# Attention stage: turn and mix moved one block behind the scores, one softmax per block, PSUM banks shared out anew

## The chip, the cores and the metric

The kernel runs on one core of one Trainium2 chip. The metric is the device time of one execution in microseconds (us), lower is better; three runs of the kernel before were timed. TensorE (PE) has two clock levels here, 2.4 GHz (granted clock 1.00 in the views) and 1.2 GHz (0.50).

## What is computed

Two encoders feed an attention over N = 4 states for each of 1024 tokens; an interference stage and three dense layers follow. The attention stage is what the change touches:

```python
# TOK = 1024 tokens, N = 4 states, D = 512, H = 8 heads of HD = 64
qr = heads(sr @ Wq_r.T + bq_r); qi = heads(si @ Wq_i.T + bq_i)
kr = heads(sr @ Wk_r.T + bk_r); ki = heads(si @ Wk_i.T + bk_i)
vr = heads(sr @ Wv_r.T + bv_r); vi = heads(si @ Wv_i.T + bv_i)
ar = einsum('bhnd,bhmd->bhnm', qr, kr) + einsum('bhnd,bhmd->bhnm', qi, ki)
ai = einsum('bhnd,bhmd->bhnm', qi, kr) - einsum('bhnd,bhmd->bhnm', qr, ki)
mag = sqrt(ar ** 2 + ai ** 2 + 1e-08) * HD ** (-0.5)
w = softmax(mag, axis=-1)                       # over the 4 states of one token
out_r = einsum('bhnm,bhmd->bhnd', w, vr); out_i = einsum('bhnm,bhmd->bhnd', w, vi)
attn_r = out_r @ Wo_r.T + bo_r; attn_i = out_i @ Wo_i.T + bo_i
```

## The kernel before

The program is six stages one after the other (constants, first layers, second layers, attention, interference, top), each with its own five instruction streams (TensorE = PE, VectorE = DVE, ScalarE = ACT, GpSimd = POOL, SyncE = SP) written out by hand and tied together by counting semaphores. There is no scheduler: each engine works its stream in the order in which it is written, so an instruction that waits holds up all that stands behind it on its engine.

**The attention stage** (`phase_attention`, L491) works on 16 blocks `b` of 64 tokens (256 columns: 64 tokens times 4 states). Inside a block, `m` = 0..3 stands for a pair of heads. Every dense product is made of three fp32r matmuls (`split3`, L50 to L52: high by high, low by high, high by low), and so every result that feeds another product is split into a high and a low half, by ACT and DVE. The pieces of a block are:

- `project(b, m)` on PE (lines L50 to L52 with `t_sx`): q and k for a pair of heads, 24 matmuls of 256 columns each. ACT reads q out of PSUM (`q_evac`, L618, 4 instructions), DVE reads k (`k_evac`, L708, 8 instructions).
- `values(b)`: v, four groups of 12 matmuls of 512 columns. ACT reads them out (L680).
- `score(b, m, h)` (L846): fp32 matmuls of q by k. ACT squares the result (L625).
- `softmax(b, m)` on DVE: add, mask, sum (L725, L729, L730); ACT root (L671); DVE maximum and difference (L735, L736); ACT exponent (L674); DVE sum, reciprocal (L739, L740), and the spread of the weights into `pd` (L744).
- `turn(b, m)` (L852) transposes `pd` on PE, ACT copies it out (`pt_evac`, L631), `mix(b, m)` (L865) multiplies it by v, ACT and DVE split the result (`o_high` L638, `o_low` L753).
- `project_out(b)`: the output projection (L50 to L52 with `t_ohi`), 96 matmuls, read out by `a_high` (L646, ACT) and `a_low` (L764, DVE), and stored by SP.

**Banks.** PSUM's eight banks are shared out in pairs: 0 and 1 for q, k, v and the output projection, 2 and 3 for the scores, 4 and 5 for `turn`, 6 and 7 for `mix`, so `turn` and `mix` each alternate between two banks.

**Order.** PE's body interleaves: `project(b, m+1)`, a score, `turn` of the pair before (`before(b, m)`), the second score, `mix` of the pair before; `values` and the output projection of block b-1 stand after m = 0. ACT and DVE follow in the same order. The 32 weight pieces are split into halves at the start of the stage and in block 0 (`pieces`). SP stores block b-1 before it loads block b+1 (`load_s`).

## Time and profile before

| | us |
|---|---|
| median of 3 runs | 3566.72 |
| lowest, highest | 3565.09, 3569.43 |
| span of the profiled execution | 3548.6 |
| median less that span | 18.1 |
| attention stage, first to last matmul | 1179.9 |
| one block of it | 71.6 |
| PE busy over the whole span | 3115.3 (88%) |
| DVE busy, ACT busy | 1652.0 (47%), 1168.9 (33%) |

The profiled execution's record gives its span alone and no device time of its own; the runs' median lies 18.1 us above it, for what is ahead of the first and behind the last instruction. A busy share is an average over six stages. What a change in the attention stage is worth is read from that stage, by what PE waits for in one block.

### The profile page before, as it was taken

How to read it: one execution, taken by the hardware profiler on the slowest of the kernel's cores; microseconds unless marked ns; L12 is line 12 of the kernel's file. 1: busy time of each engine (PE TensorE's matmuls, PEld its weight loads, DVE VectorE, ACT ScalarE, POOL GpSimd, SP SyncE). 2: the span in 40 equal slices, each digit the busy share in tenths (PEclk: the TensorE clock that was granted, in tenths of full speed). 3: DMA queues.
4: the chain of work that ended last, by engine and by line, in shares of the span. 5: the costliest groups of instructions: out<-in, count | busy, mean ns of one | idle time of the engine just before them, and what ended most of it. 6: DMA issues, size and time to landing. Idle time of an engine off the chain costs nothing. (4 is left out here: it accounts for less than half of the span.)

```text
span 3548.6 us, 45531 instructions
## 1 busy us (share of the span) xinstructions
PE 3115.3 (88%) x16160; PEld 2659.5 (75%) x16160; DVE 1652.0 (47%) x3027; ACT 1168.9 (33%) x1986; POOL 388.2 (11%) x345
## 2 busy tenths in 40 slices
PE   8999999996999899995889989898989598884586
PEld 6888888885888788874778878887878476763575
DVE  3222222226211341114665566556655579999322
ACT  3111111114211241114554555455555432332332
POOL 1000000001111110010000000000000244543100
PEclk9999999998999999997998989898989799997798
DMA  5222222214333333323212221122112553442210
GB/s 181 71 71 71 71 71 71 71 59 163 113 95 95 113 118 94 93 74 128 78 47 56 62 71 47 49 70 71 47 47 72 136 102 83 89 85 45 95 36 6
DMA packets 364201, 285.38 MB, mean 80 GB/s; under 512 B 280048, under 2 KB 280176, under 8 KB 364016
## 3 DMA queue, kind: packets, MB, share of 16 engines
q1 hardware_dynamic: 341488, 206.97, 21.6%
q0 software_dynamic: 22656, 77.67, 6.3%
q8 instruction: 33, 0.54, 0.1%
q14 instruction: 24, 0.20, 0.0%
HBM read 194.40 MB, written 90.18 MB: 80 GB/s over the span
## 5 line engine op out<-in xcount | busy, mean ns | idle before, releaser
L50 PE MATMUL banks<-a_whi,a_xhi 128*128 128x512 f32 x1152 | 449.9, 391 | 24.0 <-DVE a_wlo L175 17.6
L51 PE MATMUL banks<-a_wlo,a_xhi 128*128 128x512 f32 x1152 | 448.8, 390 | 0.0
L52 PE MATMUL banks<-a_whi,a_xlo 128*128 128x512 f32 x1152 | 448.8, 390 | 0.0
L50 PE MATMUL banks<-b_ghi,b_whi 128*128 128x512 f32 x1024 | 401.8, 392 | 9.9 <-DVE b_slo L383 8.6
L51 PE MATMUL banks<-b_glo,b_whi 128*128 128x512 f32 x1024 | 398.9, 390 | 0.0
L52 PE MATMUL banks<-b_ghi,b_wlo 128*128 128x512 f32 x1024 | 398.8, 389 | 0.0
L175 DVE TENSOR_TENSOR a_wlo<-a_wraw,a_whi 128x512 fp32r<-128x512 f32 x144 | 99.6, 692 | 577.2 <-ACT a_whi L161 577.2
L50 PE MATMUL banks<-t_sx,t_whi 128*128 128x256 f32 x1024 | 307.7, 300 | 36.8 <-DVE t_wlo L791 26.9
L161 ACT ACTIVATE a_whi<-a_wraw 128x512 fp32r<-128x512 f32 x144 | 90.9, 632 | 667.7 <-PE banks L52 628.9
L51 PE MATMUL banks<-t_sx,t_whi 128*128 128x256 f32 x1024 | 295.7, 289 | 0.0
L368 DVE TENSOR_TENSOR b_wlo<-b_wraw,b_whi 128x512 fp32r<-128x512 f32 x128 | 88.2, 690 | 444.8 <-ACT b_whi L320 444.6
L52 PE MATMUL banks<-t_sx,t_wlo 128*128 128x256 f32 x1024 | 294.5, 288 | 0.0
L708 DVE TENSOR_SCALAR t_ks<-banks,cols 64x256 f32<-64x256 f32 x512 | 247.4, 483 | 97.5 <-PE banks L52 86.4
L50 PEld LDWEIGHTS banks<-a_whi,a_xhi 128*128 128x128 f32 x1152 | 216.6, 188 | 72.0 <-issue 17.6
L52 PEld LDWEIGHTS banks<-a_whi,a_xlo 128*128 128x128 f32 x1152 | 216.6, 188 | 45.2
L51 PEld LDWEIGHTS banks<-a_wlo,a_xhi 128*128 128x128 f32 x1152 | 216.7, 188 | 44.8
L50 PEld LDWEIGHTS banks<-t_sx,t_whi 128*128 128x128 f32 x1024 | 203.5, 199 | 43.2 <-DVE t_wlo L791 27.5
L50 PEld LDWEIGHTS banks<-b_ghi,b_whi 128*128 128x128 f32 x1024 | 192.7, 188 | 54.9 <-DVE b_slo L383 13.1
L320 ACT ACTIVATE b_whi<-b_wraw 128x512 fp32r<-128x512 f32 x128 | 80.2, 628 | 458.2 <-PE banks L52 457.5
L50 PE MATMUL banks<-i_whi,i_ax 128*128 128x512 f32 x384 | 159.3, 415 | 72.6 <-ACT i_ng L1075 38.1
L52 PEld LDWEIGHTS banks<-b_ghi,b_wlo 128*128 128x128 f32 x1024 | 192.4, 188 | 40.1
L51 PEld LDWEIGHTS banks<-b_glo,b_whi 128*128 128x128 f32 x1024 | 192.7, 188 | 39.0
(192 smaller groups left out, 6208.8 us busy)
## 6 DMA issues: line engine op xcount, KB each, us to landing
a_wraw<-w_first SPq DMA_DIRECT2D x144, 256.0 KB, 2.6
b_wraw<-w_second SPq DMA_DIRECT2D x128, 256.0 KB, 2.7
t_sx<-s_scr SPq DMA_DIRECT2D x64, 512.0 KB, 5.5
a_scr<-t_at SPq DMA_DIRECT2D x256, 128.0 KB, 1.9
i_ax<-a_scr SPq DMA_DIRECT2D x64, 512.0 KB, 5.9
h_scr<-a_hst POOLq DMA_DIRECT2D x72, 256.0 KB, 2.7
b_hl<-h_scr POOLq DMA_DIRECT2D x16, 1024.0 KB, 6.0
s_scr<-b_shi POOLq DMA_DIRECT2D x32, 512.0 KB, 4.4
```

Of the source, the lines that this page charges most:

```text
L50: mm(out, ahi, bhi, start=first, stop=False)
L51: mm(out, ahi, blo, start=False, stop=False)
L52: return mm(out, alo, bhi, start=False, stop=last)
L161: act.activation(whi[:, k % SPL, :], wraw[:, k % RAW, :], ACT.Copy).then_inc(w_hi, 1)
L175: dve.tensor_tensor(wlo[:, k % SPL, :], wraw[:, k % RAW, :], whi[:, k % SPL, :].bitcast(F32), ALU.subtract).then_inc(w_split, 1)
L320: act.activation(whi[:, j % SPL, :, :].rearrange("p a n -> p (a n)"), wraw[:, j % RAW, :], ACT.Copy).then_inc(w_hi, 1)
L368: dve.tensor_tensor(wlo[:, j % SPL, :, :].rearrange("p a n -> p (a n)"), wraw[:, j % RAW, :], whi[:, j % SPL, :, :].bitcast(F32).rearrange ...
L708: ins = dve.tensor_scalar(ks[half(at_half), m % 2, h, part, :], b_qk[half(h), 1, e * C:(e + 1) * C], bcol(M_K + e, m, half(h)), float(sign ...
```

## The change

The reference is computed as before, with the same matmuls.

- **Banks.** Bank 0 alone for q, banks 1 and 2 for k, 3 and 4 for the scores, bank 5 alone for both `turn` and `mix` (`b_pm`), banks 6 and 7 for v and the output projection.
- **One block behind.** `turn` and `mix` of block b-1 run among the projections and scores of block b. In body b: projection of q, `turn(b-1, m-1)`, projection of k, `score(b, m-1)`, `mix(b-1, m-1)`, for m = 1..3; then `turn(b-1, 3)`, the first values, the last score, `mix(b-1, 3)`, the other values, and the output projection of b-1.
- **One softmax a block.** `softmax` falls apart: `pick` (add, mask, sum) for each pair of heads, then once a block `magnitude`, `shift`, `exponent` and `total` for all four pairs at once, and `spread` for each pair.
- **New waits.** `turn(b, m)` waits for `o_split` of the pair before it, since `mix` of that pair was read out of the same bank.
- **The end.** The last block's four turns and mixes run after the loop, one after the other.
- SP loads block b+1 ahead of the stores of block b-1, in two halves. GpSimd clears 11 old semaphores at the start of the second layers.

```diff
-        b_qk, b_sc, b_pt, b_mx = (g.ps[:, 2 * i:2 * i + 2, :] for i in range(4))
+        b_q = g.ps[:, 0, :]
+        b_k = g.ps[:, 1:3, :]
+        b_sc = g.ps[:, 3:5, :]
+        b_pm = g.ps[:, 5, :]
+        b_vo = g.ps[:, 6:8, :]
...
             def turn(b, m):
-                pe.wait_ge(step, b * 32 + (8 * m + 8))
+                pe.wait_ge(pd_made, b * 4 + (m + 1))
+                if not isinstance(b, int) or 4 * b + m >= 1:
+                    pe.wait_ge(o_split, b * 8 + 2 * m)
```

PE's body, which takes the place of the old one:

```diff
+            def body(b, first):
+                project(b, 0, 0)
+                project(b, 0, 1)
+                for m in range(1, KD):
+                    project(b, m, 0)
+                    if not first:
+                        turn(b - 1, m - 1)
+                    project(b, m, 1)
+                    score(b, m - 1)
+                    if not first:
+                        mix(b - 1, m - 1)
+                if not first:
+                    turn(b - 1, KD - 1)
+                values(b, 0)
+                score(b, KD - 1)
+                if not first:
+                    mix(b - 1, KD - 1)
+                for i in range(1, 4):
+                    values(b, i)
+                if not first:
+                    project_out(b - 1)
```

DVE's body:

```diff
+            def body(b, first):
+                k_evac(b, 0)
+                for m in range(1, KD):
+                    k_evac(b, m)
+                    pick(b, m - 1)
+                    if not first:
+                        spread(b - 1, m)
+                        o_low(b - 1, m - 1)
...
+                pick(b, KD - 1)
+                if not first:
+                    o_low(b - 1, KD - 1)
+                shift(b)
+                total(b)
+                spread(b, 0)
+                if not first:
+                    for m in range(KD):
+                        a_low(b - 1, m)
```

ACT's body up to the third pair, and PE's end of the stage:

```diff
+            def body(b, first):
+                q_evac(b, 0)
+                for m in range(1, KD):
+                    q_evac(b, m)
+                    if not first:
+                        pt_evac(b - 1, m - 1)
+                    square(b, m - 1)
+                    if not first:
+                        o_high(b - 1, m - 1)
+                    if first and m == 1:
+                        pieces(M_V * KD, M_O * KD)
+                    if first and m == 3:
+                        pieces(M_O * KD, NP)
...
             blocks(pe, body)
-            turn(NB - 1, KD - 1)
-            mix(NB - 1, KD - 1)
+            for m in range(KD):
+                turn(NB - 1, m)
+                mix(NB - 1, m)
             project_out(NB - 1, True)
```

DVE's stream before, in block 1 at the pair m = 1 (`t_olo` is the low half of the mixed result, `t_ks` the k read-out, `t_m` and `t_sc` the softmax's steps, `t_pd` the spread weights; x7 counts like instructions):

```order
313 L753 SCALAR_TENSOR_TENSOR t_olo<-banks,cols,t_ohi 64x256 [waits t_o_hi]
314 L753 SCALAR_TENSOR_TENSOR t_olo<-banks,cols,t_ohi 64x256 x3
315 L708 TENSOR_SCALAR t_ks<-banks,cols 64x256 [waits t_scored,t_projected]
316 L708 TENSOR_SCALAR t_ks<-banks,cols 64x256 x7
```

The low half of a pair stands right ahead of the next k read-out, and nothing that PE does on the way asks for it but a `mix` two pairs later.

DVE's stream after the change, in block 1 between one k read-out and the next:

```order
329 L749 TENSOR_SCALAR t_ks<-banks,cols 64x256 [waits t_projected,t_scored]
330 L749 TENSOR_SCALAR t_ks<-banks,cols 64x256 x7
331 L759 TENSOR_TENSOR t_m<-t_sq 128x512 [waits t_picked,t_squared]
332 L764 TENSOR_TENSOR t_m<-t_m,mask 128x512 [waits t_summed]
333 L768 TENSOR_REDUCE t_mg<-t_m 128x16 [waits t_mag_done,t_masked]
334 L798 SCALAR_TENSOR_TENSOR t_pd<-t_ex,t_inv,mask 128x128 [waits t_p_turned,t_inv_done]
335 L798 SCALAR_TENSOR_TENSOR t_pd<-t_ex,t_inv,mask 128x128 x3
336 L807 SCALAR_TENSOR_TENSOR t_olo<-banks,cols,t_ohi 64x256 [waits t_o_hi]
337 L807 SCALAR_TENSOR_TENSOR t_olo<-banks,cols,t_ohi 64x256 x3
```

The low half now stands last, behind the k read-out, the pick and the spread.

PE's stream before, in block 0 around the last two pairs of scores (`t_ks,t_qs` the scores, `ident,t_pd` the turn, `t_ptl,t_v` the mix):

```order
1912 L846 MATMUL banks<-t_ks,t_qs 128x2x128 [waits t_squared,t_k_read,t_q_read]
1913 L846 MATMUL banks<-t_ks,t_qs 128x2x128
1914 L852 MATMUL banks<-ident,t_pd 128x128 [waits t_step]
1915 L852 MATMUL banks<-ident,t_pd 128x128 x3
1916 L846 MATMUL banks<-t_ks,t_qs 128x2x128 [waits t_squared]
1917 L846 MATMUL banks<-t_ks,t_qs 128x2x128
1918 L865 MATMUL banks<-t_ptl,t_v 128x128 [waits t_v_read,t_pt_read]
1919 L865 MATMUL banks<-t_ptl,t_v 128x128 x3
```

The turn waits for its weights alone (`t_step`).

PE's stream after the change, in block 1 at the last turn:

```order
2126 L905 MATMUL banks<-t_ks,t_qs 128x2x128 [waits t_squared,t_k_read,t_q_read]
2127 L905 MATMUL banks<-t_ks,t_qs 128x2x128
2128 L905 MATMUL banks<-t_ks,t_qs 128x2x128 [waits t_squared]
2129 L905 MATMUL banks<-t_ks,t_qs 128x2x128
2130 L924 MATMUL banks<-t_ptl,t_v 128x128 [waits t_v_read,t_pt_read]
2131 L924 MATMUL banks<-t_ptl,t_v 128x128 x3
2132 L913 MATMUL banks<-ident,t_pd 128x128 [waits t_o_split,t_pd_made]
2133 L913 MATMUL banks<-ident,t_pd 128x128 x3
2134 L50 MATMUL banks<-t_whi,t_sx 128x512 [waits t_v_read,t_w_split]
```

Here the turn of the last pair follows at once on the mix of the pair before, and waits for `t_o_split` too; the 512-column values stand behind it.

## Rows read from the trace of the kernel before

**Rows 1.** Windows view: length, busy us of PE, PEld, DVE, ACT, POOL; PEclk; DMA.

```profile
1618.18:2798.04 1179.86, 1037.10 (x6656) 936.92 (x6656) 707.79 (x1748) 636.85 (x1174) 0.00 (x0) 0.90 0.21 59
1860.90:1932.54 71.64, 64.44 (x416) 58.32 (x416) 43.34 (x108) 38.97 (x72) 0.00 (x0) 0.90 0.22 59
```

**Rows 2.** Timeline of ACT: first values read-out of blocks 3 and 4.

```profile
1860.90 1.08 ACT L680 ACTIVATE t_v<-banks 128x512 f32<-128x512 f32 x2
...
1932.54 1.08 ACT L680 ACTIVATE t_v<-banks 128x512 f32<-128x512 f32 x2
```

**Rows 3.** Timeline of PE in one block: start, us, instruction, [idle before <-releaser].

```profile
1861.55 0.79 PE L50 MATMUL banks<-t_whi,t_sx 128*128 128x512 f32 x1 [3.14 <-ACT t_v L680]
...
1869.71 0.39 PE L52 MATMUL banks<-t_whi,t_sx 128*128 128x512 f32 x1
1869.94 0.28 PE L50 MATMUL banks<-t_ohi,t_whi 128*128 128x256 f32 x1
...
1881.25 0.28 PE L50 MATMUL banks<-t_sx,t_whi 128*128 128x256 f32 x1
...
1887.00 1.03 PE L846 MATMUL banks<-t_ks,t_qs 128*128 128x256 f32 x4
1887.87 0.60 PE L852 MATMUL banks<-ident,t_pd 128*128 128x128 f32 x4
1888.30 1.03 PE L846 MATMUL banks<-t_ks,t_qs 128*128 128x256 f32 x4
1889.23 1.16 PE L865 MATMUL banks<-t_ptl,t_v 128*128 128x128 f32 x8
1890.14 0.36 PE L50 MATMUL banks<-t_sx,t_whi 128*128 128x256 f32 x1
...
1903.28 3.78 PE L846 MATMUL banks<-t_ks,t_qs 128*128 128x256 f32 x8 [2.43 <-DVE t_ks L708]
```

**Rows 4.** Waits of PE from 1840 to 2760 us: total, times, longest.

```profile
PE banks L50 <- ACT t_v L680: 40.8, 13, 3.2
PE banks L846 <- DVE t_ks L708: 29.1, 12, 2.4
PE banks L865 <- ACT t_ptl L631: 15.6, 13, 1.2
```

**Rows 5.** Timeline of DVE in the same block.

```profile
1887.20 4.02 DVE L708 TENSOR_SCALAR t_ks<-banks,cols 64x256 f32<-64x256 f32 x8 [3.43 <-PE banks L52]
...
1895.78 1.14 DVE L744 SCALAR_TENSOR_TENSOR t_pd<-t_sc,mask 128x128 f32<-128x128 f32 x4
1897.11 2.00 DVE L753 SCALAR_TENSOR_TENSOR t_olo<-banks,cols,t_ohi 64x256 fp32r<-64x256 f32 x4 [0.18 <-ACT t_ohi L638]
1899.13 4.02 DVE L708 TENSOR_SCALAR t_ks<-banks,cols 64x256 f32<-64x256 f32 x8
1903.18 0.69 DVE L725 TENSOR_TENSOR t_m<-t_sq 128x512 f32<-128x512 f32 x1
...
1904.64 0.69 DVE L730 TENSOR_REDUCE t_sc<-t_m 128x16 f32<-128x512 f32 x1
```

**Rows 6.** Timeline of PE in the last stage: a gap, and the matmuls behind it.

```profile
3393.57 0.55 PE L50 MATMUL banks<-e_whi,e_rhi 128*128 128x256 f32 x1 [4.58 <-DVE e_rlo L1496]
...
3396.70 0.31 PE L52 MATMUL banks<-e_whi,e_rlo 128*128 128x256 f32 x1
```

**Rows 7.** Timeline of PE at the end of the attention stage.

```profile
2776.92 1.12 PE L852 MATMUL banks<-ident,t_pd 128*128 128x128 f32 x4 [4.00 <-DVE t_pd L744]
...
2784.89 0.55 PE L50 MATMUL banks<-t_ohi,t_whi 128*128 128x256 f32 x1 [4.09 <-issue]
```

**Rows 8.** Timeline of PE at the start of the stage, in block 0.

```profile
1625.79 0.58 PE L50 MATMUL banks<-t_sx,t_whi 128*128 128x256 f32 x1 [2.88 <-DVE t_wlo L791]
...
1647.08 0.79 PE L50 MATMUL banks<-t_whi,t_sx 128*128 128x512 f32 x1 [7.90 <-DVE t_wlo L791]
```

**Rows 9.** DMA issues: KB each, median us to landing.

```profile
t_sx<-s_scr SPq DMA_DIRECT2D x64, 512.0 KB, 5.5
```

More of the change, by code:

```diff
@@ L76, in phase_constants @@
         cols_in = s.sem("cols_in")
+        g.spent = [zeroed, made, cols_in]
         block = s.ctx.enter_context(nc.Block())
@@ L288, in load_h @@
                 pool.dma_start(hl[:, j % 2, :, :], src.rearrange("t p f -> p t f")).then_inc(h_loaded[j % 2], 16)
+            for old in g.spent:
+                pool.sem_clear(old)
             load_h(0, 0)
@@ L604, in _ @@
                 sp.dma_start(raw(i), g.w_pieces[PC_ATT + i]).then_inc(w_loaded[i % TR], 16)
-            blocks(sp, body)
+            reload(0)
+            reload(1)
+            store(0)
+            with sp.Fori(2, NB - 1) as b:
+                reload(b)
+                store(b - 1)
+            store(NB - 2)
             store(NB - 1)
@@ L709, in k_evac, with pick @@
                                                 bcol(M_K + e, m, half(h)), float(sign), ALU.add, ALU.mult)
                     ins.then_inc(k_read, 1)
-            def softmax(b, m, unit=None):
-                done = [0]
-                def link(ins):
-                    ins.then_inc(step, 1)
-                    done[0] += 1
-                    dve.wait_ge(step, b * 32 + (8 * m + done[0]))
+            def pick(b, m):
                 dve.wait_ge(squared, b * 8 + (2 * m + 2))
+                if not isinstance(b, int) or 4 * b + m >= 1:
+                    dve.wait_ge(picked, b * 4 + m)
@@ L768, in a_low @@
                     ins.then_inc(a_split, 1)
-            def before(b, m):
-                return (b, m - 1) if m else (b - 1, KD - 1)
-            def body(b, first, last):
-                for m in range(KD):
-                    if m < KD - 1:
-                        k_evac(b, m + 1)
-                    if first and m == 0:
-                        pieces(M_V * KD, M_O * KD)
-                    if first and m == 2:
-                        pieces(M_O * KD, NP)
-                    softmax(b, m, (b + 1, 0) if m == KD - 1 and not last else None)
-                    if not (first and m == 0):
-                        o_low(*before(b, m))
-                    if m == 0 and not first:
-                        for mm in range(KD):
-                            a_low(b - 1, mm)
             def pieces(i0, i1):
@@ L792, in pieces @@
                                       ALU.subtract).then_inc(w_split, 1)
+            def body(b, first):
[6 more added lines that the diff above has]
+                        o_low(b - 1, m - 1)
+                    if first and m == 1:
+                        pieces(M_V * KD, M_O * KD)
+                    if first and m == 3:
+                        pieces(M_O * KD, NP)
+                pick(b, KD - 1)
[5 more added lines that the diff above has]
+                if not first:
+                    for m in range(KD):
+                        a_low(b - 1, m)
             pieces(0, M_V * KD)
-            k_evac(0, 0)
             blocks(dve, body)
-            o_low(NB - 1, KD - 1)
+            for m in range(KD):
+                if m < KD - 1:
+                    spread(NB - 1, m + 1)
+                o_low(NB - 1, m)
             for m in range(KD):
@@ new lines, in values @@
+            def values(b, i):
+                pe.wait_ge(w_split, M_O * KD)
+                e, gr = i // 2, i % 2
+                if i >= 2:
+                    pe.wait_ge(v_read, b * 4 + (i - 1))
+                elif not isinstance(b, int) or b >= 2:
+                    pe.wait_ge(a_split, b * 8 - (10 - 2 * i))
+                elif b == 1:
+                    pe.wait_ge(v_read, 3 + i)
+                for k in range(KD):
+                    w = (M_V + e) * KD + k
+                    mm = split3(pe.matmul, b_vo[:, i % 2, :], sx[:, e, 0, gr, k, :], sx[:, e, 1, gr, k, :],
+                                whi[:, w, :], wlo[:, w, :], k == 0, k == KD - 1)
+                mm.then_inc(v_full, 1)
@@ new lines, in score @@
+            def score(b, m):
+                pe.wait_ge(q_read, b * 8 + (2 * m + 2))
+                pe.wait_ge(k_read, b * 16 + (4 * m + 4))
+                for h in range(2):
+                    if not isinstance(b, int) or 4 * b + m >= 1:
+                        pe.wait_ge(squared, b * 8 + (2 * m - 1 + h))
+                    for gr in range(NG):
+                        cols = slice(gr * P, (gr + 1) * P)
+                        out = b_sc[:, h, :].rearrange("p (a g c) -> p a g c", a=2, g=NG)[:, :, gr]
+                        mm = pe.matmul(out, qs[:, m % 2, h, cols], ks[:, m % 2, h, :, cols], start=True, stop=True)
+                    mm.then_inc(scored, 1)
```

307 lines of the change are left out of this document (144 added, 163 removed).

## The prediction, made before the changed kernel was run

> **What bounds the kernel now.** I read the page first, for the shares: PE is busy 88% of the span, DVE 47%, ACT 33%. That is a mean over six stages, so I went on to the windows view of the attention stage alone. It takes 1179.9 us from its first matmul to its last, with PE busy for 1037.1 and a granted clock of 0.90 [rows 1]. All sixteen blocks look alike: the first values read-out of one block stands 71.64 us behind that of the block before [rows 2]. So I cut out one such block. PE is busy 64.4 us of it and idle for 7.2, at a clock of 0.90 [rows 1].
>
> PE's timeline shows what a block holds at the upper clock level [rows 3]. Two projections and so 48 matmuls of 256 columns take 1881.25 to 1887.00, 5.75 us, or 2.88 for q and 2.88 for k alone. Half of a pair's scores is 0.87, a turn 0.43 (1887.87 to 1888.30), a mix 0.91 (1889.23 to 1890.14). The output projection is 1869.94 to 1881.25, 11.3. The 512-column matmuls of the values stand 0.23 apart (1869.71, 1869.94), so 48 of them are 10.9. The sum for a block is 8 x 2.88 + 8 x 0.87 + 4 x 0.43 + 4 x 0.91 + 10.9 + 11.3 = 57.5 us. The remaining 14.1 are 7.2 of idle time and 6.9 in which PE works at half clock.
>
> The view of the waits names the idle time [rows 4]: about 3.1 us a block for ACT's values read-out, 2.4 for the k read-out ahead of the last scores, 1.2 for ACT's copy of the turned weights. Behind the 3.14 us gap the 24 matmuls of the values take 1861.55 to 1869.94, 8.4 us in place of 5.45 [rows 3], which is PE at 1.2 GHz until shortly before their end; the rest of the 6.9 comes behind the other two waits, where eight score matmuls take 3.78 us. So the block is bound by PE, plus waits on DVE and ACT, plus the slow clock that follows each wait. This is what a change of order can win, or lose.
>
> **The change part by part.**
>
> *The three old waits* go. The values no longer share banks with q and k and stand behind a long run of PE work; the first two groups find free banks, and the v read-outs are no longer queued behind a softmax's two table loads. The copy of the turned weights has a whole k projection (2.88 us) to hide in, where 0.87 us of scores hid it. That would take 7.2 us of idle and 6.9 of slow clock off each block, if nothing took their place.
>
> *The new wait.* Turn and mix now share bank 5. `turn(b-1, m)` may write only when DVE has done `o_low` of the pair before. I walk DVE's queue from the moment T at which PE has issued its last matmul of a k projection. DVE starts its k read-out 0.20 later (1887.00 against 1887.20, [rows 3, 5]). The read-out's eight instructions take 4.05 (1899.13 to 1903.18), the pick 2.19 (three of 0.73), the spread 1.17 (1.14 and a step), `o_low` 2.02 (1897.11 to 1899.13) [rows 5], and I add 0.07 for the hand-over to PE. The turn can start at T + 9.7. In the same time PE has: two halves of scores 1.74, mix 0.91, the next q projection 2.88, so 5.53. It waits 9.7 - 5.5 = 4.2 us for the second turn and as much for the third. Ahead of the fourth turn there is no q projection, so PE has 2.65 of work and waits 7.05. What is queued behind it on PE is the k projection in the first two cases (and DVE's next k read-out waits for that, so the gap can't be made up), the values in the third. Sum: 4.2 + 4.2 + 7.0 = 15.4 us idle a block, for 7.2 before.
>
> *The clock.* Each of these gaps is longer than the 3.14 us one, behind which PE ran slow for most of 8.4 us and lost 2.9 [rows 3]. The other bound is the 4.58 us gap in the last stage: the matmuls behind it are slow from 3393.57 to 3396.70 [rows 6], 15 of them 0.21 apart in place of 0.12, so 1.4 lost. I take 2.3 a gap, between the two and nearer to the first, which lies in this stage. Three gaps: 6.9 us a block, with 4.2 and 8.4 as ends.
>
> *One softmax a block.* It takes six of eight table loads and most of the small steps off ACT and DVE. DVE is busy 43.3 us of a block and ACT 39.0 [rows 1], less than a block of 57.5. The load was not the bound, the order is. Worth nothing beside the above. The once-a-block steps wait for each other while PE has 8.2 us of values and 11.3 of output projection to do; they need four small DVE steps of under 0.3 each and two table loads on ACT, about 5 us together.
>
> *SP.* Block b+1's second half is loaded when the last values are done and lands in about 5.5 us [rows 9], under 11.3 us of output projection. If that cover were gone it would cost its excess, microsecond for microsecond, once a block. The stores queue behind four issues, and their first data comes later than that anyway.
>
> *Block 0.* It has no turns and mixes: 8 x 2.88 + 6.96 + 10.9 = 40.9 of work. Before, it had waits for weight pieces of 2.88 and 7.90 [rows 8], and others. Now the values come last, so the 7.90 goes; the first 2.9 stays; I expect about 4 where the q read-out stands behind eight pieces on ACT, and about 4 where the v read-outs stand behind the last eight. With 4 for the clock: 56.
>
> *The end.* The four turns and mixes of block 15 have nothing beside them. The chain turn, copy, mix, `o_high`, `o_low` is in the trace once: from the turn at 2776.92 to the first matmul of the output projection at 2784.89, 7.97 us at the lower clock [rows 7]. Four of them are 32, and the output projection 13.2 with a slow start (it took 2784.89 to 2798.04). So 45.
>
> *The 11 cleared semaphores* stand ahead of the second layers' first load. No row shows such an instruction on GpSimd; between 0 and 1 us, I take 0.5.
>
> **The sum.** A block: 57.5 + 15.4 + 6.9 = 79.8 us, for 71.6. The stage: 56 + 15 x 79.8 + 45 = 1298, for 1179.9. With the 0.5: 119 us more. The trace's span of 3548.6 becomes 3667, and with the 18.1 us by which the median lies above the span, 3686 us.
>
> **The rivals.**
>
> *The bank wait is hidden (faster).* The mechanism would be that `o_low` is done before PE comes to the turn. It decides at 5.5 us for two of the turns and 2.65 for the third. Then all waits are gone, a block is 57.5, and the stage 56 + 863 + 45 = 964: 216 less, 3351 us. For it: DVE has only some 40 us of work in a block. Against it: the walk gives 9.7, the k read-out alone takes 4.05 of it, and DVE works in order. The Trainium skill (TensorE: Matmul & The Clock Gate, HAM oscillation) reports of one kernel that double-buffering PSUM brought no further gain once its loop kept PE fed; by that, one bank in place of two and two would cost nothing, and this rival's time would come out. No row of this trace shows two engines sharing a single bank in turns. 4 in 100.
>
> *The clock stays up (no change).* If gaps of 4 and 7 us did not lower the clock, the 15 x 6.9 us and some 12 at the ends fall away: 3571 us, 0.1% from now. The new idle time alone would then be what the old idle time and slow clock were together. For it: nothing but that the pattern of work differs. Against: the gap of 3.14 us was followed by slow matmuls, 13 times in the stretch of [rows 4] at the same place. 5 in 100.
>
> *The load comes late.* If the second half of the next block's data took 13 us in place of 5.5, the first projections would wait 2 us in 15 blocks: 3716 us. 4 in 100.
>
> *The slow clock lasts.* With the gaps about every 13 us, PE may stay at half clock through the first values too, another 2 to 3 us a block: 3725 us. 4 in 100.
>
> **How the numbers follow.** My forecast has 83 in 100. Its own bounds: the clock from 4.2 to 8.4 a block is -40 and +22 us; the walk's durations, by 0.3 in each of three gaps, 14; block 0 and the end 8. That makes 3635 to 3722. The range 3620 to 3725 takes in the late load and leaves out the rivals at 3351 and 3571. Faster by over 0.2% has 4 in 100 (the first rival); within 0.2%, which is about what a measurement of this kernel can tell from no change, 5 (the second); slower by over 0.2% has 91.
>
> **What would show it right or wrong.** The profile after should show PE idle before the turn (L913), with `o_low` (L807) as releaser, three times a block from block 1 on, at some 4.2, 4.2 and 7.0 us; values read-outs 80 us apart; no wait of the values for L677 over 1 us; DVE going from k read-out to `o_low` without a gap; and four waits of some 4 us each for `o_low` at the end of the stage. The clock in one block should be near 0.8. I would be wrong if DVE's chain has gaps in it (then slower still), if the third wait is not the longest, or if the matmuls behind the waits run at 0.12 us apart.

## The result: slower by 3%, at the place that the walk named

| | before | after |
|---|---|---|
| median of 4 runs, us | 3566.01 | 3673.91 |
| lowest, highest | 3565.09, 3569.43 | 3672.49, 3677.1 |
| ratio after / before | | 1.0331, 95% interval 1.0273 to 1.039 |
| span of the profiled execution | 3548.6 | 3671.2 |
| attention stage | 1179.9 | 1286.4 |
| one block of it | 71.6 | 78.5 |

The time, 3673.91, lies inside the range of 3620 to 3725 and 12 us under the forecast of 3686. The ratio of the table is an estimate from the single runs with its interval, and not the quotient of the two medians, which is 1.030. Each later ratio is to the runs of the kernel before that were timed beside it.

**The stage and one block.** The windows view of the kernel after, for the attention stage and for one block; the columns are those of [rows 1].

```profile
1620.68:2907.12 1286.44, 1035.28 (x6656) 967.77 (x6656) 673.07 (x1556) 506.42 (x982) 0.00 (x0) 0.88 0.20 54
1903.42:1981.93 78.51, 64.05 (x418) 60.01 (x417) 41.17 (x96) 30.87 (x60) 0.00 (x0) 0.89 0.20 53
```

PE is busy as long as before, 64.05 us of a block against 64.44 in [rows 1], and idle for 14.5 where it was idle for 7.2. DVE and ACT have less to do than before (41.17 for 43.34, 30.87 for 38.97). Less work on both, and a longer block: its length is not set by the amount of their work.

**The old waits went, and one new one came.** First PE's costliest idle group on the page, then the view of the waits from 1840 to 2760 us (total, times, longest), the window of [rows 4].

```profile
L913 PE MATMUL banks<-ident,t_pd 128*128 128x128 f32 x256 | 62.9, 393 | 229.9 <-DVE t_olo L807 229.9
```

```profile
DVE t_ks L749 <- PE banks L52: 200.8, 48, 6.2
...
PE banks L913 <- DVE t_olo L807: 173.6, 36, 6.7
...
PEld banks L50 <- ACT t_v L677: 3.5, 11, 0.3
```

The three waits of [rows 4] (the values on L680, the scores on L708, the mix on L631) have no row for PE any more; the values' weight load waits 0.3 us once a block. In their place stands one wait, of `turn` (L913) for `o_low` (L807). And DVE, which PE waits for, waits 48 times itself, up to 6.2 us, for the k projection. The two wait for each other in turns. That has the look of a ring, not of an overloaded engine; the first experiment below tells the two apart.

**The ring, link by link.** Timeline of DVE in one pair of the kernel after (start, us, instruction, [idle before <-releaser]):

```profile
2104.30 4.02 DVE L749 TENSOR_SCALAR t_ks<-banks,cols 64x256 f32<-64x256 f32 x8 [4.92 <-PE banks L52]
2108.35 0.69 DVE L759 TENSOR_TENSOR t_m<-t_sq 128x512 f32<-128x512 f32 x1
2109.08 0.69 DVE L764 TENSOR_TENSOR t_m<-t_m,mask 128x512 f32<-128x512 f32 x1
2109.80 0.69 DVE L768 TENSOR_REDUCE t_mg<-t_m 128x16 f32<-128x512 f32 x1
2110.41 1.13 DVE L798 SCALAR_TENSOR_TENSOR t_pd<-t_ex,t_inv,mask 128x128 f32<-128x128 f32 x4
2111.57 2.00 DVE L807 SCALAR_TENSOR_TENSOR t_olo<-banks,cols,t_ohi 64x256 fp32r<-64x256 f32 x4
```

And of PE beside it, from the last matmul of the q projection on:

```profile
2109.47 0.28 PE L52 MATMUL banks<-t_sx,t_wlo 128*128 128x256 f32 x1
2113.62 1.12 PE L913 MATMUL banks<-ident,t_pd 128*128 128x128 f32 x4 [3.87 <-DVE t_olo L807]
2114.39 0.56 PE L50 MATMUL banks<-t_sx,t_whi 128*128 128x256 f32 x1
```

DVE runs from its k read-out at 2104.30 to the end of `o_low` at 2113.57 without a gap, and PE's turn starts 0.05 later. PE had run out of work at 2109.75. The next k projection is queued behind the turn, and DVE's next k read-out waits for that.

### The profile page after: what moved, and what is told of

It is laid out like the page before. It is cut to its first block and busy times, and to the rows that moved or that the text cites. A ratio compares the mean times of both kernels' runs of the same rounds, so it can differ in the third digit from the quotient of the medians.

```text
span 3671.2 us, 44702 instructions
## 1 busy us (share of the span) xinstructions
PE 3111.7 (85%) x16160; PEld 2688.5 (73%) x16160; DVE 1616.9 (44%) x2835; ACT 1038.2 (28%) x1794; POOL 389.0 (11%) x345
## 5 line engine op out<-in xcount | busy, mean ns | idle before, releaser
L749 DVE TENSOR_SCALAR t_ks<-banks,cols 64x256 f32<-64x256 f32 x512 | 247.4, 483 | 280.2 <-PE banks L52 270.3
L50 PE MATMUL banks<-t_sx,t_whi 128*128 128x256 f32 x1024 | 324.0, 316 | 34.5 <-DVE t_wlo L827 27.0
L51 PE MATMUL banks<-t_sx,t_whi 128*128 128x256 f32 x1024 | 313.7, 306 | 0.0
L52 PE MATMUL banks<-t_sx,t_wlo 128*128 128x256 f32 x1024 | 312.0, 305 | 0.0
L913 PE MATMUL banks<-ident,t_pd 128*128 128x128 f32 x256 | 62.9, 393 | 229.9 <-DVE t_olo L807 229.9
L50 PEld LDWEIGHTS banks<-t_sx,t_whi 128*128 128x128 f32 x1024 | 224.2, 219 | 35.8 <-DVE t_wlo L827 27.6
L51 PEld LDWEIGHTS banks<-t_sx,t_whi 128*128 128x128 f32 x1024 | 222.9, 218 | 0.1
```

The costliest lines, as they stand in the source:

```text
L50: mm(out, ahi, bhi, start=first, stop=False)
L51: mm(out, ahi, blo, start=False, stop=False)
L52: return mm(out, alo, bhi, start=False, stop=last)
L749: ins = dve.tensor_scalar(ks[half(at_half), m % 2, h, part, :], b_k[half(h), m % 2, e * C:(e + 1) * C], bcol(M_K + e, m, half(h)), float(s ...
L913: mm = pe.transpose(b_pm[:, x * P:(x + 1) * P], pd[:, x, :, :].rearrange("p n b -> p (n b)"), g.ident[:, :])
```

## The experiments

All are edits of the changed kernel, but for one run of the kernel before. The rows that begin with "and" each keep the edits of the row above them. The diffs are cut to the lines that matter (`...`); comments in them explain a line. The table puts the results together; the sections below it have the reasons. The block is the mean distance of the fourth turns of successive blocks; idle is the sum of PE's gaps in one block; "slow" is what is left of the block after 57.5 us of work and the idle time.

| kernel | median, us | block | idle | slow | stage |
|---|---|---|---|---|---|
| after | 3673.9 | 78.5 | 14.5 | 6.5 | 1286.4 |
| extra DVE work behind `o_low` | 3677.4 | 78.5 | 14.5 | 6.5 | 1285.9 |
| extra DVE work ahead of `o_low` | 3741.1 | 82.7 | 18.0 | 7.2 | 1351.2 |
| gaps filled with matmuls | 3604.3 | 73.8 | 3.9, and 10.6 of filling | 1.8 | 1216.3 |
| `o_low` ahead of pick | 3542.9 | 69.9 | 8.3 | 4.1 | 1157.0 |
| spread first, `o_low` ahead of pick | 3521.5 | 68.4 | 7.8 | 3.0 | 1134.4 |
| two banks for turn and mix | 3561.9 | 71.7 | 9.4 | 4.8 | 1176.6 |
| two banks and the new order | 3409.1 | 61.5 | 3.0 | 1.0 | 1023.5 |
| and mix ahead of the scores | 3401.5 | 60.9 | 2.6 | 0.9 | 1015.8 |
| and exponential behind the values | 3400.4 | 60.9 | 2.5 | 0.9 | 1013.5 |
| and values' read-outs first | 3349.2 | 58.4 | 0.8 | 0.1 | 978.0 |
| before, traced again | 3566.4 | 71.7 | 7.2 | 6.9 | 1181.8 |

### Is `o_low` the last link? Extra work ahead of it and behind it

```diff
                         spread(b - 1, m)
+                        idle_work(b, m)   # two reductions of 128x512 to an unread tile
                         o_low(b - 1, m - 1)
```

> The changed kernel with two extra VectorE reductions a pair (128 x 128 elements to a tile that nobody reads, some 0.7 us each, an extra of this experiment) between spread and o_low, in three pairs of every block but the first. My theory (o_low ends the chain that the turn waits for): each of the three gaps grows by the whole 1.4 us, a block by 4.2 to 5.5 us with the clock that follows, the whole 3674 -> 3735 to 3755 us. Rival (VectorE is waiting anyway and o_low is not the last link): 3670 to 3685 us.

```diff
                         spread(b - 1, m)
                         o_low(b - 1, m - 1)
+                        idle_work(b, m)
```

> The same two extra VectorE reductions a pair with an unread result as in the run before, but behind o_low. VectorE waits there for the next k projection (48 waits of k_evac in the stage), so by my theory they cost nothing as long as that wait is longer than 1.4 us: 3670 to 3680 us. Rival (VectorE is busy enough that any work on it costs, wherever it stands, because its own load or its shared port sets the block): the same increase as the run before, 3735 us or more.

Ahead of it (ratio to before 1.0511, interval 1.0465 to 1.0557), the timeline of DVE and the view of PE's waits from 1840 to 2760 us:

```profile
2117.76 1.27 DVE L836 TENSOR_REDUCE t_junk<-mask 128x16 f32<-128x512 f32 x2
```

```profile
PE banks L924 <- DVE t_olo L809: 198.4, 33, 7.9
```

Behind it (1.0328, 1.0282 to 1.0374), the same view, which is that of after to 0.1 us:

```profile
PE banks L924 <- DVE t_olo L809: 173.7, 36, 6.7
```

The two reductions take 1.27 us. Ahead of `o_low` each of the three gaps grew by 1.19 (3.87 to 5.05 and 5.06, 6.74 to 7.93), the block by 4.2 and the whole by 67 us. Behind it the same instructions cost nothing in the stage (1285.9 for 1286.4). The 3.5 us between the medians lie behind the stage: what follows it takes 768.1 us in both kernels with the extra work and 764.1 in the changed kernel. Why was not tried; some 4 of the 67 us are of that kind, and the stage has the other 65. So DVE's load does not set the block; its chain up to `o_low` does. The rival of a busy DVE falls.

### What the gaps cost beside their length: filling them

```diff
                         if m > 1:
+                            fill(b, 24)   # matmuls of 256 columns into an idle bank, unread
                         turn(b - 1, m - 1)
...
                 if not first:
+                    fill(b, 40)
                     turn(b - 1, KD - 1)
```

> The changed kernel with extra TensorE work whose result is unused, put into the gaps: 24 matmuls of 256 columns ahead of the turns of the second and third pair of a block, 40 ahead of the last turn, into a bank that is idle there. At the full clock they take about 0.12 us each, 2.9 and 4.8 us, less than the gaps of 3.87 and 6.74. Nothing else moves. My theory (6.5 of a block's 78.5 us are PE at its lower clock level behind the gaps): the turns start where they started, the time behind them runs at the full clock, the granted clock of the stage rises from 0.88 to 0.95 or more, a block takes 72 to 74 us and the whole 3674 -> 3585 to 3610 us, though PE does more work. Rival A (the clock is an effect of something else, or fill that is issued late delays the turn): 3674 us or more, up to 3674 + 15 x 1 = 3690. Rival B (part of it: the filling keeps the clock only behind the short gaps): 3625 to 3660 us.

Measured 3604.26 us, ratio 1.0164 (1.006 to 1.0268). The windows view of the stage, and PE's waits from 1840 to 2760 us:

```profile
1619.70:2835.97 1216.27, 1123.41 (x7976) 1057.79 (x7976) 672.34 (x1552) 505.52 (x981) 0.00 (x0) 0.97 0.21 57
```

```profile
PE banks L913 <- DVE t_olo L807: 49.2, 38, 2.0
```

PE does 1320 matmuls more and the kernel is 70 us faster. The gaps of 3.87, 3.87 and 6.74 are now 0.98, 0.99 and 1.95 us of waiting behind 24, 24 and 40 matmuls at 0.12 us: 2.9, 2.9 and 4.8, so the turns wait no less than before. What changed is the clock behind them: granted 0.97 for 0.88, and 4.7 us a block less. That is the price of the clock alone, measured with the waits in place, and times 15 blocks it gives the 70 us. It is a demonstration and no remedy; the order and the banks below take the gaps away.

### Which part of the chain: the order on DVE, and the bank

```diff
-                    pick(b, m - 1)
                     if not first:
                         spread(b - 1, m)
                         o_low(b - 1, m - 1)
+                    pick(b, m - 1)
```

> The changed kernel with one change of order on VectorE: spread(b-1, m) and o_low(b-1, m-1) stand ahead of pick(b, m-1) in place of behind it. Banks and all other orders as in the changed kernel. My theory: pick (three operations, about 2.2 us) leaves the chain that the turn waits for; the gaps at the turn fall from 3.87, 3.87, 6.74 to about 1.7, 1.7, 4.6 us, and with them part of the 6.5 us that PE loses a block to the half clock. A block 66 to 72 us, the whole 3480 to 3575 us. What could be late next is ScalarE's next square, which needs the sums of pick: a wait of PE at score(b, m) would show it. Rival A (the order on VectorE has no part in the block's length, since the turn waits for ScalarE's o_high): 3665 to 3680 us. Rival B (pick becomes late and the scores wait instead): gaps move to the scores, 3600 to 3680 us.

```diff
+                    if not first:
+                        spread(b - 1, m)
                     k_evac(b, m)
-                    pick(b, m - 1)
                     if not first:
-                        spread(b - 1, m)
                         o_low(b - 1, m - 1)
+                    pick(b, m - 1)
...
-                pick(b, KD - 1)
                 if not first:
                     o_low(b - 1, KD - 1)
+                pick(b, KD - 1)
```

> The changed kernel with the order of VectorE alone rewritten: spread(b-1, m), k_evac(b, m), o_low(b-1, m-1), pick(b, m-1), and o_low(b-1, 3) ahead of pick(b, 3). Banks as in the changed kernel. spread then fills the time in which VectorE waits for the k projection, and only k_evac (4.2 us of read-outs, of which the part behind the projection counts) and o_low are left in the chain to the turn. My theory: gaps of about 1.4, 1.4 and 4.3 us, of which part no longer lowers the clock, a block of 65 to 70 us, the whole 3460 to 3550 us. Rival (the bank alone decides and order gives only what taking pick out gave): as the run with spread and o_low ahead of pick, within 10 us.

```diff
-        b_k = g.ps[:, 1:3, :]
-        b_pm = g.ps[:, 5, :]
+        b_k = g.ps[:, 1, :]
+        b_pm = g.ps[:, 2:6:3, :]     # turn and mix of pair m in [:, m % 2, :]
...
-                if not isinstance(b, int) or 4 * b + m >= 1:
-                    pe.wait_ge(o_split, b * 8 + 2 * m)
+                if not isinstance(b, int) or 4 * b + m >= 2:
+                    pe.wait_ge(o_split, b * 8 + (2 * m - 2))
...
-                elif not isinstance(b, int) or 4 * b + m >= 2:
-                    pe.wait_ge(k_read, b * 16 + (4 * m - 4))
+                elif not isinstance(b, int) or 4 * b + m >= 1:
+                    pe.wait_ge(k_read, b * 16 + 4 * m)
```

The last lines are the price: k has one bank now, and its projection waits for the read-out of the pair before.

> The changed kernel with another share-out of the same banks: k is projected into bank 1 alone, and turn and mix alternate between banks 2 and 5 (bank 2 was k's second), so that turn(b-1, m) waits only for the read-outs of mix(b-1, m-2). The order of every engine is the changed kernel's. My theory (the turn waits 3.87, 3.87 and 6.74 us a block because it stands behind o_low in the same bank, and o_low behind k_evac, pick and spread on VectorE): the wait on o_low goes, but the turn still needs its own spread weights, which VectorE makes right ahead of o_low, so some 1.8 to 2.1 us remain at each of the first two and 4.7 to 5.0 at the last, and k's single bank adds about 1 us at one or two k projections. A block 78.5 -> 68 to 74 us, the whole 3674 -> 3510 to 3600 us. Rival A (the shared bank is the whole cause): no wait at the turn, a block of 57.5 to 60 us, 3360 to 3400 us. Rival B (the bank has no part in it; the order on VectorE or the clock sets the block): 3665 to 3680 us. Rival C (k's single bank costs more than the second turn bank gives): over 3680 us.

Measured: 3542.93 us (ratio 0.9954, 0.993 to 0.9978), 3521.46 (0.9939, 0.9895 to 0.9983) and 3561.88 (1.0015, 0.9982 to 1.0049). PE's waits with `o_low` ahead of pick, from 1840 to 2740 us:

```profile
PE banks L913 <- DVE t_olo L807: 108.4, 39, 4.7
```

With spread first as well, from 1840 to 2700 us:

```profile
PE banks L914 <- DVE t_olo L807: 83.2, 39, 4.0
PE banks L50 <- ACT t_v L677: 18.4, 13, 1.4
```

```profile
2106.66 4.02 DVE L749 TENSOR_SCALAR t_ks<-banks,cols 64x256 f32<-64x256 f32 x8 [1.00 <-PE banks L52]
2111.24 1.99 DVE L807 SCALAR_TENSOR_TENSOR t_olo<-banks,cols,t_ohi 64x256 fp32r<-64x256 f32 x4 [0.56 <-ACT t_ohi L669]
```

With two banks in the old order, from 1840 to 2760 us, and DVE's timeline around one of the turns (PE's turn started at 2138.09):

```profile
PE banks L913 <- DVE t_pd L798: 111.0, 39, 4.8
PE banks L50 <- DVE t_ks L749: 10.4, 13, 0.8
```

```profile
2136.91 1.13 DVE L798 SCALAR_TENSOR_TENSOR t_pd<-t_ex,t_inv,mask 128x128 f32<-128x128 f32 x4
2138.07 2.00 DVE L807 SCALAR_TENSOR_TENSOR t_olo<-banks,cols,t_ohi 64x256 fp32r<-64x256 f32 x4
```

Taking pick's three steps out of the chain made the gaps 1.82, 1.82 and 4.69 us, each 2.05 shorter: just pick (2108.35 to 2110.41 in the timeline of after). Taking spread out too made them 1.18, 1.18 and 4.05, by 0.64 and not by spread's 1.13: behind the k read-out `o_low` now waits for ACT's `o_high`, which had been hidden, as DVE's timeline of that kernel shows. And with two banks the releaser of the turn is no longer `o_low` but the spread ahead of it in the queue, so the gap is shorter by `o_low`'s 2.0 alone (1.84, 1.92, 4.78), while the k projection waits 0.8 us once a block for k's single bank. In the old order, then, the second bank is worth 2 us of each gap; what is left stands behind DVE's k read-out, pick and spread. The rival of the bank as the whole cause (3360 to 3400 us) and that of a bank without a part in it (3665 to 3680) both fall.

### Both together

> Both: two banks in turn for turn and mix (2 and 5), k in bank 1 alone, and VectorE in the order spread, k_evac, o_low, pick. My theory (the two causes add up: with the wait on the bank gone and spread ahead, nothing that the turn needs is late): no gap over 1.5 us at the turns, a block of 59.5 to 62 us, the stage 990 to 1030 us, the whole 3375 to 3420 us, under the kernel before (3566). Rival A (something hidden so far ends last: the bias copies and squares of ScalarE, or k's single bank): 63 to 68 us a block, 3430 to 3510 us. [...]

Measured 3409.1 us, ratio 0.961 (0.9511 to 0.9708). Windows view of the stage, and PE's waits from 1840 to 2600 us:

```profile
1620.46:2643.93 1023.47, 952.39 (x6656) 885.51 (x6656) 674.65 (x1556) 504.28 (x981) 0.00 (x0) 0.98 0.25 68
```

```profile
PE banks L50 <- ACT t_v L677: 27.9, 26, 1.4
PE banks L50 <- DVE t_ks L749: 9.6, 12, 0.8
```

No turn waits any more. In the block's length the two edits add up: order alone took 10.1 us, banks alone 6.8, both 17.0. Link by link they do not, and the sum is in part a coincidence. At each turn the order took away 2.7 us and the banks 2.0. From the first two gaps of 3.87 the two together can take no more than 3.87; from the third, of 6.74, they would leave 2.0, and nothing was left. The reason lies in the program: with two banks the turn waits for its spread alone, and the order puts the spread ahead of the k read-out, so the k read-out leaves the chain too, which neither edit does by itself. What PE still waits for, 2.9 us a block, is elsewhere: 0.7 and 1.4 us at the values and 0.8 at the k projection. The granted clock of the stage is 0.98, where the same two banks with the old order had 0.92:

```profile
1619.86:2796.48 1176.62, 1010.79 (x6656) 937.80 (x6656) 673.15 (x1556) 506.94 (x982) 0.00 (x0) 0.92 0.22 59
```

The next edit moves the mix ahead of the scores, and `o_high` ahead of the squares on ACT:

```diff
                     project(b, m, 1)
-                    score(b, m - 1)
                     if not first:
                         mix(b - 1, m - 1)
+                    score(b, m - 1)
```

> The run before with one more move: mix(b-1, m-1) ahead of score(b, m-1) on TensorE and o_high ahead of square on ScalarE. My theory: the read-outs of mix come 0.9 us earlier and mix no longer stands behind the scores' wait for k_evac; the k read-out is covered by the mix. A block of 59 to 60.5 us, the whole 3365 to 3400 us, 0 to 20 us under the run before. Rival (mix then waits for ScalarE's copy of the turned weights, which the scores covered): gaps at mix of about 1 us each, 4 us a block, 3430 to 3460 us.

Measured 3401.53 us, 0.9589 (0.9491 to 0.9688): 8 us less than the run before, in the direction expected, but 1.5 us above the expected range, with a block of 60.9 in place of at most 60.5. No mix waits for ACT's copy, so the rival falls.

### The last waits of the values: two misses, and the waits gone

```diff
                 v_evac(b, 1)
-                exponent(b)
                 v_evac(b, 2)
                 v_evac(b, 3)
+                exponent(b)
```

> The best kernel so far (two banks in turn, VectorE in the order spread, k_evac, o_low, pick, and mix ahead of the scores) with one more change on ScalarE: the block's exponential stands behind all four read-outs of the values in place of between the second and the third. In the kernel before it the values wait 0.36 and 1.41 us a block for the third and fourth read-out, which stand behind the exponential, which waits for VectorE. Theory: both gaps go, 60.9 -> 59.1 us a block, the whole 3401 -> 3372 to 3378 us; VectorE's sums and the first spread come 2 to 3 us later and are covered by the output projection (11.3 us). Rival: a_low, which stands behind that spread on VectorE, comes late, and the third part of the output projection waits for it: 3395 us or more.

Measured 3400.39 us: no gain, and the values' waits were still there. ACT's timeline shows why:

```profile
2092.81 0.60 ACT L677 ACTIVATE t_v<-banks 128x512 f32<-128x512 f32 x1
2093.42 1.28 ACT L684 ACT_TABLE_LOAD   x1
2097.01 0.35 ACT L684 ACTIVATE t_mag<-t_mg,tiny_hd 128x64 f32<-128x64 f32 x1 [2.31 <-DVE t_mg L768]
2097.27 1.06 ACT L677 ACTIVATE t_v<-banks 128x512 f32<-128x512 f32 x2
```

I had taken the wrong instruction for the one in the way. It is not the exponential but the square root (L684), one place earlier, which waits 2.31 us for DVE's last pick, with the second read-out behind it. The exponential stood behind a read-out that was late already. The next run moves the right one:

```diff
                 square(b, KD - 1)
+                v_evac(b, 0)
                 if not first:
                     o_high(b - 1, KD - 1)
-                v_evac(b, 0)
-                magnitude(b)
                 v_evac(b, 1)
+                magnitude(b)
```

> The kernel of the run before (exponential behind the values) with two more moves on ScalarE: the first read-out of the values ahead of o_high(b-1, 3), and the second ahead of magnitude. In the trace of the run before the two waits of the values were still there (0.34 and 1.41 us a block): the second and third read-out stood behind magnitude, which waited until 2097.01 for VectorE's last pick, and the values of block row 3 for the read-out that followed. Theory: both waits go, 60.9 -> 59.1 us a block, the whole 3400 -> 3368 to 3376 us. Rival A: magnitude and the last o_high come late in turn and with them the output projection, 3395 us or more. Rival B: only the 0.34 or only the 1.41 goes: 3378 to 3396 us.

Measured 3349.2 us, ratio 0.9467 (0.9407 to 0.9526), 19 us below the expected 3368 to 3376. PE's waits from 1840 to 2560 us have one row left:

```profile
PE banks L50 <- DVE t_ks L749: 9.5, 12, 0.8
```

Both waits of the values are gone, as expected. The block is 58.4 us, 2.6 less than the run before where 1.8 were forecast, since the slow work behind the waits went too, and 0.9 from the 57.5 us of pure work. The stage takes 978.0, 35.5 less, and that is what this edit is worth. The other 15.7 us of the difference to 3400.4 lie elsewhere: this kernel's trace lacks the stall of the next section (0.5 us in place of 20.2, with 4.5 in place of 0.4 one tile later), and what follows its stage takes 751.8 us for 765.0.

### The 18 us outside the stage: the kernel before once more

The trace of after had a gap in the interference stage that is in no row of [rows 1 to 9], and its median lay 2.7 us above its span where before's lay 17.4 above its own. PE's timeline in the first trace of before, behind the first tile of that stage (48 matmuls) and behind the second, and in that of after, behind the first:

```profile
2833.20 0.47 PE L50 MATMUL banks<-i_whi,i_ax 128*128 128x512 f32 x1 [0.47 <-DVE i_wlo L1145]
...
2848.01 0.77 PE L50 MATMUL banks<-i_whi,i_ax 128*128 128x512 f32 x1 [3.69 <-ACT i_ng L1075]
```

```profile
2961.74 0.76 PE L50 MATMUL banks<-i_whi,i_ax 128*128 128x512 f32 x1 [18.44 <-issue]
```

> The kernel before once more, unchanged, for its trace. Its median lies 17.4 us above the span of the trace that the prediction read, while the changed kernel's median lies 2.7 above its own, and the changed kernel's trace has an 18.4 us stall of TensorE, put down to issue, in the interference stage, where the trace of before had 3.7. Theory: that stall belongs to the interference stage in both kernels and was by chance short in the trace of before; then another trace of before shows a span of 3560 to 3568 us with a stall of 15 to 20 us at the first tiles of the interference stage, the attention stage again at 1180 us, and a time 2 to 3 us above its span. Rival: the changed kernel brought the stall; then the span of before is again near 3549 with about 4 us there.

Measured 3566.42 us, ratio 1.001 (0.9971 to 1.005), with a span of 3567.2. Windows view of its attention stage, and PE's timeline in the interference stage:

```profile
1620.80:2802.64 1181.84, 1038.51 (x6656) 937.98 (x6656) 707.82 (x1748) 636.87 (x1174) 0.00 (x0) 0.90 0.22 59
```

```profile
2857.92 0.77 PE L50 MATMUL banks<-i_whi,i_ax 128*128 128x512 f32 x1 [20.62 <-issue]
```

So the stall is in the kernel before as well. It stands behind the first tile in eleven of the thirteen traces of this study, at 18.4 to 20.6 us, and is absent from the first trace of before and from that of the last kernel: these have 0.5 us there, and wait 3.7 and 4.5 us for ACT behind the second tile, where the others wait under 0.5. Where the last kernel was measured, the kernel before had a median of 3548.35, for 3564.5, 3554.8 and 3564.8 in the three comparisons ahead of it, so it was short there too. The stall comes with the execution and not with the edit. Against this second trace of before, the changed kernel's whole difference is in the attention stage: 1286.4 less 1181.8 is 104.6 us, the spans differ by 104.0, and what follows the stage takes 764.6 and 764.1.

## Why the prediction was right, step by step

**The place, the releaser and the number of waits** were right. PE waits before L913 three times a block from block 1 on, released by L807, with DVE's chain closed from the k read-out to `o_low`, and the third wait the longest. The experiments show the mechanism too: `o_low` is the last link (extra work ahead of it and behind it), and pick and `o_low`, taken out of the chain one at a time, each gave back their own time.

**The gaps** were 3.87, 3.87 and 6.74 us for 4.2, 4.2 and 7.05: 0.3 too long each. From the start of its k read-out to the end of `o_low` DVE takes 9.27 us (2104.30 to 2113.57), where the walk summed 4.05 + 2.19 + 1.17 + 2.02 = 9.43; nearly all of that is pick, 2.06 for 2.19. The rest is PE's own work in the meantime, 5.65 us for 5.53 (from 2104.10, 0.20 ahead of DVE's start, to 2109.75). A walk from the durations of [rows 5] was good to 5 to 9% of each gap.

**The clock** was 6.9 a block, with 4.2 and 8.4 as ends, and came out at 6.5 (78.5 - 57.5 - 14.5). Filling the gaps brought back 4.7 of it without shortening a wait, which shows that it is the clock and nothing else that took those. The price was right as a sum. What I gave as its mark was not: I wrote that the granted clock of a block should be near 0.8, and it is 0.89, about what it was before. It could have been read from [rows 1], where 6.9 us of slow work stood beside a clock of 0.90. The figure in that column is a mean over the stretch, idle time included, and not a measure of lost time.

The same 2.3 us for every gap was a mean that hides a spread. The windows view of after takes three stretches of one block, each from the start of a turn to where the matmuls are back at the upper level; the gaps ahead of them were 3.87, 3.86 and 6.74 us.

```profile
1942.43:1945.33 2.90, 2.90 (x14) 2.90 (x15) 0.00 (x0) 0.60 (x1) 0.00 (x0) 0.50 0.00 0
1956.61:1962.40 5.79, 5.79 (x27) 5.79 (x28) 0.00 (x0) 0.60 (x1) 0.00 (x0) 0.50 0.00 0
1972.06:1976.05 3.99, 3.99 (x12) 3.31 (x13) 0.00 (x0) 0.60 (x1) 0.00 (x0) 0.50 0.00 0
```

PE works at half clock for 2.9, 5.8 and 4.0 us, and loses about half of each: an estimate of 1.4, 2.9 and 2.0, or 6.3 a block. In this block two gaps of one length differ by a factor of two, and the longest is not the dearest. Two readings on the way were off, without weight for the result. Behind the 3.14 us gap of [rows 3] the granted clock was low for 14 of the 24 matmuls, not until shortly before their end; and three times the 2.9 read there is 8.8, not 8.4. Nor do the parts of the range add up as written: 40, 14 and 8 below 3686 and 22, 14 and 8 above it make 3624 to 3730, not 3635 to 3722.

**The old waits** went as said: no row of PE for L677, L749 or L660.

**One softmax a block** was priced at nothing. DVE and ACT are busy 2.2 and 8.1 us a block less, and with 1.3 us of idle work put back on DVE behind `o_low` three times a block nothing changed in the stage. That bears the price out for DVE. For ACT it is not shown, and neither is what the one softmax is worth in a kernel whose order is good: no run split it again.

**Block 0 and the end.** 56 and 45 were forecast. PE's timeline of after, in block 0:

```profile
1651.29 0.36 PE L50 MATMUL banks<-t_sx,t_whi 128*128 128x256 f32 x1 [3.49 <-issue]
...
1671.29 0.47 PE L50 MATMUL banks<-t_whi,t_sx 128*128 128x512 f32 x1 [3.56 <-ACT t_v L677]
...
1684.11 0.58 PE L50 MATMUL banks<-t_sx,t_whi 128*128 128x256 f32 x1 [4.07 <-DMA t_sx<-s_scr]
```

and at the end of the stage:

```profile
2877.96 1.09 PE L913 MATMUL banks<-ident,t_pd 128*128 128x128 f32 x4 [4.14 <-DVE t_olo L807]
2879.74 2.07 PE L924 MATMUL banks<-t_ptl,t_v 128*128 128x128 f32 x8 [0.69 <-ACT t_ptl L660]
2885.94 1.08 PE L913 MATMUL banks<-ident,t_pd 128*128 128x128 f32 x4 [4.14 <-DVE t_olo L807]
```

The end is right: turns 7.98 us apart where [rows 7] gave 7.97, though only three turns wait there, and the fourth wait, of 4.09, is that of the output projection. Block 0 took 59.4 and another 4.07 in which block 1 waits for its data. That wait was missed. The SP paragraph priced the load of the next block against 11.3 us of output projection as cover, and block 0 has no output projection. The prediction could have seen it, since it says itself what the load costs when that cover is gone.

**The sum.** 15 blocks are 15 x (79.8 - 78.5) = 19.5 us less than forecast, block 0 and the end 7.5 more: 1286.4 for 1298. The stage should have cost 118 over the first trace's 1179.9 and cost 106.5, or 104.6 against the second trace. No run shows the 0.5 us for the cleared semaphores; at that size it is lost in the differences between executions: the stage began at 1618.18 and 1620.80 us in the two traces of before, and at 1620.68 in that of after.

**The 18.1 us "around the span"** was the step that was wrong in kind. I took what lies between a trace's span and the median of other runs for a fixed piece ahead of the first and behind the last instruction. A run's time is 2 us above its own span (3673.26 us for 3671.2). Of the other 16, the stall makes 14: what follows the stage takes 750.6 us in the first trace of before and 764.6 in the second. The first trace lacked it by chance. The sum came out because the stall is in the median of both kernels, so adding 18.1 carried it along under another name. That part of the sum was luck: nothing in the prediction said that the changed kernel would have the stall.

**The rivals.** The hidden wait (3351 us) failed as the walk said: DVE came to the end of `o_low` 3.87 us too late. The Trainium skill (TensorE: Matmul & The Clock Gate, HAM oscillation) reports that PSUM double-buffering gave one kernel no further gain. Taken as a rule, one bank for turn and mix would have been as good as two. Here the second bank was worth 6.8 us a block in the old order and 6.9 in the new, 112 us of the whole (3521.5 to 3409.1, and 3673.9 to 3561.9), so it does not carry over to this bank, for which two engines wait on each other. The clock that stays up (3571) fell to the slow matmuls behind every gap. Of the late load one instance came, behind block 0. The slow clock that lasts through the values did not come: 6.5 us a block leave no room for another 2 to 3.

The price of that rival was sound all the same: a stage of 964 us with every wait hidden. The last kernel has 978.0, with blocks of 58.4 for 57.5. What the rewrite's count of work promised is there; the order on DVE and ACT and the share-out of banks kept it out of reach.

## What to carry to other kernels

When a change takes three waits away and puts two users into one bank, walk the queue of the engine that frees the bank from the last event that it depends on, and add up all that stands ahead of the freeing instruction, whatever it is for. The first remedy is the order of that queue: put what the waiting engine needs first, and what nobody waits for soon (here pick, 2.06 us) last. And before a time is laid beside a span, look whether the same execution gave both.

## What the runs showed of the hardware

- **The clock is a price of its own on a gap.** With the turns as late as before and most of the gaps filled by unused matmuls, 4.7 of the 6.5 us a block came back. In the changed kernel the first matmuls behind a 3.87 us gap are 0.21 us apart (granted clock 0.50), those from 1945.42 on 0.12:

```profile
1942.43 1.11 PE L913 MATMUL banks<-ident,t_pd 128*128 128x128 f32 x4 [3.87 <-DVE t_olo L807]
1943.20 0.56 PE L50 MATMUL banks<-t_sx,t_whi 128*128 128x256 f32 x1
...
1945.05 0.41 PE L52 MATMUL banks<-t_sx,t_wlo 128*128 128x256 f32 x1
1945.26 0.32 PE L50 MATMUL banks<-t_sx,t_whi 128*128 128x256 f32 x1
1945.42 0.28 PE L51 MATMUL banks<-t_sx,t_whi 128*128 128x256 f32 x1
```

- **A stall of 18 to 21 us that comes and goes with the execution.** PE has nothing to wait for that the trace shows. SP and ACT do wait for PE, by the program for its semaphores `a_used` and `multiplied`, and start again 0.4 us ahead of PE's own next matmul at 2961.74:

```profile
2961.35 1.75 SPq L1039 DMA_DIRECT2D i_ax<-a_scr  x2
2961.36 0.60 ACT L1133 ACTIVATE i_mag<-banks 128x512 f32<-128x512 f32 x1 [9.64 <-remote]
```

  So it seems that PE's signals for the tile that it had done came only at the end of the stall, which points between its last matmul and those signals, where the program has a `drain`, and not at the data of the next tile. It is in eleven of thirteen traces, always behind the first tile of the interference stage, and between the two traces of the kernel before it makes 14 of the 18.6 us by which their spans differ. Its cause was not tried and stays open.
- **Short runs of the kernel before.** Among its repeated runs are some at 3515 to 3548 us, 20 to 50 us below the rest. Each run has its mean granted clock: 0.938 to 0.949 in those, 0.929 to 0.934 in the runs at 3560 to 3571. They spend less time at the lower clock level. None of them was traced, so why is open; they make the intervals of the ratios wide.
